# New slot tables for the state-space layer of a two-layer network on one Trainium2 core: 32 half slots, other row pairs on GpSimd, its row copies at other places

## What is computed

```python
def _ssm_forward(x, in_proj_w, conv_w, conv_b, x_proj_w, dt_proj_w, dt_proj_b, A_log, D_param, out_proj_w):
    ...
    h = _silu(h.transpose(0, 2, 1))            # after a causal convolution of 4 taps
    x_dbl = h @ x_proj_w
    dlt, Bm, Cm = (x_dbl[..., :dt_rank], x_dbl[..., dt_rank:dt_rank + n], x_dbl[..., dt_rank + n:])
    delta = jax.nn.softplus(dlt @ dt_proj_w + dt_proj_b)
    deltaA = jnp.exp(jnp.einsum('bld,dn->bldn', delta, A))
    deltaB_u = (delta * h)[..., None] * Bm[:, :, None, :]
    def step(state, t):
        dA_t, dBu_t, c_t = t
        state = dA_t * state + dBu_t
        y_t = jnp.einsum('bdn,bn->bd', state, c_t)
        return (state, y_t)
    ...
    y = ys.transpose(1, 0, 2) + h * D_param
    y = y * _silu(res)
    return y @ out_proj_w
```

## Time and profile before

| | |
|---|---|
| time, median of 3 runs | 4811.3 us (4810.6 to 4814.64) |
| profiled execution, its own time | 4813.99 us |
| span of the profile (first to last instruction) | 4812.0 us |
| the third phase, first to last slot table | about 4087 to 4812 us |
| one step of the loop | 41.0 us |
| in such a step: VectorE, TensorE, ScalarE, GpSimd busy | 36.2, 35.9, 30.1, 19.7 us |

### The profile page before, as it was taken

How to read it: one execution, slowest core, us unless ns; L and a number is a source line. 1 busy time by engine, 2 the same in 40 slices (tenths; PEclk the granted TensorE clock), 3 DMA queues, 4 the chain that set the end, 5 groups by cost and what they waited for, 6 DMA issues and landing times. The chain is left out here.

```text
span 4812.0 us, 130689 instructions
## 1 busy us (share of the span) xinstructions
PE 4274.3 (89%) x45166; PEld 3170.2 (66%) x45166; DVE 3900.2 (81%) x6890; ACT 3764.5 (78%) x11543; POOL 3537.5 (74%) x2504
## 2 busy tenths in 40 slices
PE   6988699998999899998999989999899997688887
PEld 3555477776777777776777767777677776355553
DVE  4776788888888888888888888888888885588887
ACT  2555588888888888888888888888888886677774
POOL 0100799988899888998989988899899995344444
PEclk9999799999999999999999999999999998788888
DMA  1000111111111111111111111111121111000000
GB/s 26 6 5 2 50 48 44 44 38 53 52 44 38 50 45 53 38 44 44 51 47 44 44 44 46 52 43 39 44 53 44 38 44 28 2 4 3 3 3 5
DMA packets 118630, 169.29 MB, mean 35 GB/s; under 512 B 26563, under 2 KB 44422, under 8 KB 118022
## 3 DMA queue, kind: packets, MB, share of 16 engines
q1 hardware_dynamic: 109246, 160.92, 12.6%
q10 hardware_dynamic: 8776, 0.45, 0.1%
HBM read 20.79 MB, written 2.10 MB: 5 GB/s over the span
## 5 line engine op out<-in xcount | busy, mean ns | idle before, releaser
L1375 POOL TENSOR_TENSOR b_w<-b_w,b_vt 128x512 f32<-128x512 f32 x768 | 1158.3, 1519 | 317.4 <-DVE b_vt L1289 191.6
L1379 POOL TENSOR_TENSOR b_rn<-b_ssm,all_neg_half 128x16 f32<-128x16 f32 x384 | 1261.4, 3285 | 32.0
L1174 ACT ACTIVATE b_Pr<-ps,b_nm 128x96 f32<-128x96 f32 x3072 | 1002.6, 353 | 0.6
L1174 ACT ACTIVATION_READ_ACCUMULATOR b_Pr<-ps,b_nm 128x1 f32 x3072 | 677.2, 220 | 0.0
L1216 ACT ACTIVATE b_PT<-ps 96x512 f32<-96x512 f32 x768 | 457.9, 596 | 259.8 <-PE ps L1026 244.1
L1060 PE MATMUL ps<-b_Whi,b_xlo 128*128 128x512 f32 x1152 | 581.2, 505 | 47.9 <-DVE b_Wlo L1306 24.9
L989 PE MATMUL ps<-all_ident,b_w 128*128 128x128 f32 x3072 | 464.2, 282 | 134.8 <-ACT b_qkT L1144 65.9
L1287 DVE TENSOR_TENSOR b_w<-ps,until_b_rotab 128x512 f32<-128x512 f32 x768 | 525.0, 684 | 60.9 <-ACT b_sq L1193 57.2
L1026 PE MATMUL ps<-all_ident,b_Pr 128*96 128x128 f32 x3072 | 488.5, 283 | 82.3 <-ACT b_PT L1216 44.2
L1193 ACT ACTIVATE b_sq<-ps 128x512 f32<-128x512 f32 x768 | 476.3, 620 | 59.7 <-PE ps L1062 49.1
L1289 DVE TENSOR_TENSOR b_vt<-ps,until_b_rotab 128x512 f32<-128x512 f32 x768 | 523.0, 681 | 0.0
(11 more groups left out here) (259 smaller groups left out, 9403.8 us busy)
## 6 DMA issues: line engine op xcount, KB each, us to landing
b_V<-b_Vraw SPq DMA_DIRECT2D x384, 192.0 KB, 2.6
b_V<-b_Vraw SPq DMA_DIRECT2D x384, 128.0 KB, 2.3
b_V<-b_Vraw SPq DMA_DIRECT2D x192, 64.0 KB, 2.2
b_Wraw<-in_L_ffn_Wqkv SPq DMA_DIRECT2D x36, 256.0 KB, 3.4
b_Wo<-in_L_ffn_Wo SPq DMA_DIRECT2D x6, 512.0 KB, 4.1
a_xtok<-in_L_attn_hidden_states SPq DMA_DIRECT2D x16, 128.0 KB, 2.1
out<-c_xout SPq DMA_DIRECT2D x16, 128.0 KB, 1.8
b_W<-in_L_ffn_W SPq DMA_DIRECT2D x6, 341.0 KB, 3.3
```

Source lines behind the costliest of these rows:

```text
L1174: last = nc.scalar.activation(s.Pr[:, r % 2, j, i], ps[:, S_BANK[j], i * KEYS:(i + 1) * KEYS], ACT.Exp, bias=s.nm[:, r, j, i:i + 1], accum ...
L1375: nc.gpsimd.tensor_tensor(rows, rows, s.vt[:, i % 4], ALU.add).then_inc(s.pool_add, 1)
L1379: nc.gpsimd.tensor_tensor(s.rn[:, j], s.ssm[:, j], g.neg_half[:, 0:HB], ALU.pow).then_inc(s.pool_r, 1)
```

## The change

All engines now run over 32 slots (`C_SLOTS`), and every table is new. GpSimd takes the pairs B0, B2, B4, C2, C3, C4 instead of B0, B3, B4, C1, C3, C4; six products as before. TensorE's waits ahead of B0, B1, C0 and C1 are new: they wait for the product of pair 6 or 7 of the item before. No operation is added or dropped, so what changes is the order on each engine. By the tables and the order of the `if` statements the new orders of a whole step are:

- VectorE: x3, B1, xbc, B3, scan 0, delta/du, moments 1, y, C0, x4, B5, C1, B6, B7, moments 2, scan 1, C5, C6, C7, x5. Before: B1, x3, xbc, B2, scan 0, delta/du, y, moments 1, C0, x4, B5, moments 2, B6, B7, C2, scan 1, C5, C6, x5, C7.
- GpSimd: B0, B2, statistics 1, copy of x3, B4, C2, statistics 2, C3, C4. Before: B0, B3, statistics 1, B4, C1, copy of x3, statistics 2, C3, C4.
- ScalarE: rows B0, dlt, rows B2, z, softplus, out, x3, rows B4, 4 exponentials, apply 1, rows C2, hT, 6 exponentials, x4, 10 exponentials, apply 2, xp, 8 exponentials, rows C3, hT2, rows C4, 4 exponentials, silu, lin. Before, apply 2 stood behind 20 exponentials as well, with xp, hT2 and rows C3 right behind it, and then 7 exponentials, lin, rows C4.
- TensorE: B0, B1, B2, xd, B3, sum 4', B4, sum 5', dl, sum 6', sum 7', B5, out, C0, x3, B6, C1, op, C2, h, x4, B7, in, sum 0, sum 1, C3, C4, h2, conv, sum 2, C5, C6, lin, sum 3, C7 (sums with a prime are those of the item before). Before: B0, B1, xd, B2, B3, sum 4', sum 5', sum 6', B4, dl, C0, out, x3, B5, sum 7', B6, op, C1, C2, x4, h, B7, sum 0, sum 1, in, C3, h2, lin, C4, C5, conv, sum 2, C6, C7, sum 3.

```diff
 PAIRS = NS // 2
-POOL_B, POOL_C = (0, 3, 4), (1, 3, 4)
+C_SLOTS = 32
+POOL_B, POOL_C = (0, 2, 4), (2, 3, 4)
...
-PE_B = {0: (0, 1), 1: (2, 3), 3: (4,), 8: (5,), 9: (6,), 10: (7,)}
-PE_C = {6: (0,), 9: (1, 2), 11: (3,), 12: (4, 5), 13: (6, 7)}
-PE_SUM = {10: (0,), 11: (1,), 13: (2,), 14: (3,), 17: (4, 5), 18: (6,), 24: (7,)}
-PE_OUT, PE_XD, PE_X3, PE_DL, PE_OP, PE_X4, PE_H, PE_IN, PE_H2, PE_CONV, PE_LIN = 7, 0, 7, 3, 9, 9, 10, 11, 11, 12, 12
-DVE_B_AT = {0: (1,), 3: (2,), 7: (5,), 8: (6, 7)}
-DVE_C_AT = {6: (0,), 11: (2,), 13: (5, 6), 15: (7,)}
-DVE_SCAN = {4: 0, 12: 1}
-DVE_X3, DVE_XD, DVE_Y, DVE_STATS1, DVE_X4, DVE_DELTA, DVE_STATS2, DVE_X5 = 3, 3, 5, 6, 7, 5, 8, 13
-ACT_ROWS = {0: (0,), 1: (1,), 3: (2,), 9: (3,), 12: (4,), 15: (5,)}
-ACT_OUT, ACT_X3, ACT_Z, ACT_SOFTPLUS, ACT_X4, ACT_APPLY1, ACT_HT, ACT_XP, ACT_APPLY2, ACT_HT2, ACT_SILU, ACT_DLT, ACT_LIN = 2, 2, 1, 2, 10, 6, 11, 11, 11, 11, 15, 0, 15
-FACTOR_SLOT = {4: (0, 2), 10: (2, 8), 11: (8, 20), 12: (20, 27), 15: (27, 32)}
-POOL_AT = {1: (0, 1), 5: (2,), 9: (3,), 13: (4,), 14: (5,)}
-POOL_X3, POOL_STATS1, POOL_STATS2 = 12, 1, 12
+PE_B = {1: (0, 1, 2), 2: (3,), 3: (4,), 10: (5,), 17: (6,), 20: (7,)}
+PE_C = {11: (0,), 17: (1,), 18: (2,), 22: (3, 4), 23: (5,), 25: (6,), 31: (7,)}
+PE_SUM = {21: (0,), 22: (1,), 23: (2,), 30: (3,), 34: (4,), 37: (5,), 40: (6,), 41: (7,)}
+PE_OUT, PE_XD, PE_X3, PE_DL, PE_OP, PE_X4, PE_H, PE_IN, PE_H2, PE_CONV, PE_LIN = 11, 1, 16, 7, 18, 19, 19, 20, 22, 22, 28
+DVE_B_AT = {8: (1,), 10: (3,), 19: (5,), 22: (6,), 23: (7,)}
+DVE_C_AT = {14: (0,), 20: (1,), 28: (5, 6), 29: (7,)}
+DVE_SCAN = {11: 0, 27: 1}
+DVE_X3, DVE_XD, DVE_Y, DVE_STATS1, DVE_X4, DVE_DELTA, DVE_STATS2, DVE_X5 = 4, 10, 13, 13, 16, 12, 26, 29
+ACT_ROWS = {0: (0,), 2: (1,), 6: (2,), 15: (3,), 28: (4,), 30: (5,)}
+ACT_OUT, ACT_X3, ACT_Z, ACT_SOFTPLUS, ACT_X4, ACT_APPLY1, ACT_HT, ACT_XP, ACT_APPLY2, ACT_HT2, ACT_SILU, ACT_DLT, ACT_LIN = 5, 5, 2, 5, 20, 14, 15, 22, 22, 28, 30, 1, 31
+FACTOR_SLOT = {7: (0, 2), 12: (2, 4), 19: (4, 10), 21: (10, 20), 23: (20, 26), 27: (26, 28), 30: (28, 32)}
+POOL_AT = {0: (0,), 1: (1,), 21: (2,), 27: (3,), 29: (4,), 31: (5,)}
+POOL_X3, POOL_STATS1, POOL_STATS2 = 12, 5, 28
...
                     for i in PE_B.get(slot, ()) if step.states else ():
                         if i == 0:
                             pe.wait_ge(s.xd_ready, 2 * n + 2)
-                        if i >= 2 and i - 2 in POOL_B:
-                            pe.wait_ge(s.rows_ready, N_POOL * n + POOL_B.index(i - 2) + 1)
-                        elif i >= 2:
-                            pe.wait_ge(s.bu_dve, len(DVE_B) * n + DVE_B.index(i - 2) + 1)
+                        before, of = (i - 2, n) if i >= 2 else (PAIRS + i - 2, n - 1)
+                        if before in POOL_B:
+                            wait(pe, s.rows_ready, N_POOL * of + POOL_B.index(before) + 1)
+                        else:
+                            wait(pe, s.bu_dve, len(DVE_B) * of + DVE_B.index(before) + 1)
...
```

More of the change, by code:

```diff
@@ L1516, in body @@
                     copy_mod(s.md_tail, 1, known(t), 2, 6).then_inc(s.md_tail_ready, 1)
-                for slot in range(SLOTS):
+                for slot in range(C_SLOTS):
                     if step.inner and slot == DVE_STATS1:
@@ L1738, in body @@
                         last.then_inc(s.op_full, 1)
-                    for at, item, there in ((slot, n, step.states), (slot + SLOTS, t, step.tail)):
+                    for at, item, there in ((slot, n, step.states), (slot + C_SLOTS, t, step.tail)):
                         for i in PE_SUM.get(at, ()) if there else ():
@@ L1747, in body @@
                                 for c in range(CC):
-                                    nc.tensor.matmul(ps[:, Y_BANK, c * NT:(c + 1) * NT], s.D_diag[:, c], s.h[:, own if at < SLOTS else other, c], start=False, stop=False, skip_group_check=True)
+                                    nc.tensor.matmul(ps[:, Y_BANK, c * NT:(c + 1) * NT], s.D_diag[:, c], s.h[:, own if at < C_SLOTS else other, c], start=False, stop=False, skip_group_check=True)
                             if i == PAIRS - 1:
@@ L1768, in body @@
                     for i in PE_C.get(slot, ()) if step.states else ():
[L1769 to L1772, removed]
+                        before, of = (i - 2, n) if i >= 2 else (PAIRS + i - 2, n - 1)
+                        if before in POOL_C:
+                            wait(pe, s.rows_ready, N_POOL * of + len(POOL_B) + POOL_C.index(before) + 1)
+                        else:
+                            wait(pe, s.yc_dve, len(DVE_C) * of + DVE_C.index(before) + 1)
                         spread(C_BANK[i % 2], 1, i).then_inc(s.c_full, 1)
```

## The result

The changed kernel takes 4971.5 us (median of 4 runs, 4968.14 to 4977.95) against 4811.95 us before (4 runs): a ratio of 1.0325, 95% interval 1.0313 to 1.0338. It is 160 us slower. The forecast was 4923 us, 111 more than before, with a range up to 4965. The sign came as forecast, and so did the lock that the forecast named as the cause; the size was 48 us short. The profiled execution took 4977.95 us, with a span of 4976.0, which is 6.5 above the median.

The account below looks back on a forecast made before the run. No engine was full: a 41.0 us step was taken as a ring of waits. Steps of 9.8 + 0.1 + 20.6 + 18.4 = 48.9 us added 112 with the end steps, giving 4923 us, range 4870 to 4965.

Parts of the forecast that it names:

- the lock: Scan 1 holds SBUF against GpSimd's second norm, ready 9.8 us after scan 1 starts; with its stall 85%.
- end of scan 0 to scan 1: VectorE from delta to scan 1: 9.8 us of unchanged work plus 0.1 idle.
- scan 1 to C5: VectorE's C5 begins 20.6 us after scan 1; 17.4 with full clock throughout, 21.6 with a late clock.
- C5 to scan 0: VectorE does C5 (1.2 us), then 8.07 of work as before; C7 waits 0.45 for TensorE.
- Rival 1: GpSimd's four norm instructions all get through between scan 1's two instructions: step 42.5 us, time 4833; chance 6%.
- rival 2: Faster, as scan 1 begins late enough to miss the norm: step 39.0 to 40.1 us, time about 4790; chance 5%.
- Who waits: ScalarE's apply 2 waits 7.5 us for the norm, TensorE stands at h2, and the convolution takes 7 at half clock.
- the upper bound: Half clock at the out projection, late clock behind sum 2 and the second path: 10.3 us a step, time 4958.
- The second path: TensorE's B3 spread waits for the B1 product, with softplus behind it: costs 0 to 0.3 us a step.
- x4: VectorE idle ahead of x4, as y begins later and only C0 fills the time: 0.1 to 1.2 us, 0.1 taken.
- The sum: A step grows 7.8 us to 48.9; 13 steps give 101, step 14 about 8, the last about 3: together 112.

Follow-up runs that it names:

- one entry: The kernel before with only VectorE's second moments moved directly ahead of scan 1 (slot 12 for 8): 4934.6 us.
- The fills: The changed kernel with unread matrix products in TensorE's gaps, 8 ahead of B3, 3 ahead of B6, 11 ahead of h2: 4911.95 us.
- the fills and the moments together: The changed kernel with moments 2 ahead of B6 and unread matrix products ahead of B3 (8) and B6 (3), none ahead of h2: 4868.1 us.
- the three moves: The changed kernel with moments 2 ahead of B6, B1 ahead of x3 and x5 ahead of C7: 4845.6 us, ratio 1.0069.

## Why the forecast was right in sign and short in size

| stretch, us | forecast | after, two steps in turn |
|---|---|---|
| end of scan 0 to scan 1 | 9.9 | 13.46, 14.81 |
| scan 1 to C5 | 20.6 | 18.25, 18.53 |
| C5 to scan 0 | 9.7 | 11.44, 11.45 |
| scan 0 | 8.7 | 8.74, 8.74 |
| step | 48.9 | 51.9, 53.5 |

The last row adds up the column; from scan 1 to scan 1, which takes the first stretch of the next step, the trace has 53.2 and 52.4.

**The lock: right, with other instructions held.** The forecast had L332 and L333 held. In the rows L332 always passed, and L333 with L335, or L335 with L337, were held, as the scan began 0.20 or 0.33 us late. The time came out nearly the same: the norm was to be ready 9.8 us after the scan's start, or 9.0 if the scan was late by 0.2 to 0.4; it was ready at 9.5 and 8.7. Rival 1 (all four between the two scan instructions) and rival 2 (the lock misses the norm) did not happen, except that one step of ten came near to rival 2. The runs show it both ways: one entry costs the kernel before 120 us, and moments 2 moved back by four slots take 86 from the changed one.

**Who waits: right, and somewhat too long.** Apply 2 waited 7.2 (7.5 forecast), C5 9.50 (9 to 13 forecast). The convolution was taken at half clock throughout, 7 us; it took 5.04 and 6.10, since the clock came back in the middle of it. This and the norm make the way from scan 1 to C5 (c in the forecast) 18.4 instead of 20.6: the forecast charged 2.2 us a step too many here. Its own terms also add up otherwise than it wrote: 11.4 + 7 + 1.9 + 0.6 is 20.9, and with sum 2 at half clock too (3.8) it is 22.8, where the upper bound took 21.6. So redone, the upper bound lies some 16 us higher, near 4974, above the measured time; but it would have got there by a stretch that in fact came out shorter.

**The second path: the step that failed.** The forecast named it, B3's spread waiting for the B1 product with sum 4', dl, z and softplus behind, and gave it "0 to 0.3". It had added up these instructions at the durations of before, at full clock. But TensorE stands idle 3.91 us ahead of that spread, and what follows it first runs at half clock: from B3's spread (4340.53) to z (4348.22) passed 7.7 us where 5.2 were taken, and in the step after (4392.42 to 4401.35), where the clock came back later, 8.9. With 5.4 for z to softplus, the 10.6 became 13.1 and 14.3, and delta waited 2.2 and 3.5. The fills confirm it: with the clock at 1.00 this wait is 0.46. The forecast asked of the long stall whether the clock would fall, and not of this second wait that the change adds on the same engine.

**x4: mis-sized by choice.** The bounds were 0.1 to 1.2 us and 0.1 was taken. It was 1.16: the out projection ran at half clock (2.04 us, as in the earlier trace rows). Together with the second path and the scan's own start this stretch came 3.6 and 4.9 us longer than forecast.

**C5 to scan 0: a term left out.** "What lay between C6 and scan 0 before, 8.07" took over x5 at 0.48 and md_tail at its short duration. GpSimd's B0 product now runs beside both, and they take 1.19 and 1.00 (VectorE's rows of after stand above): the stretch is 1.7 us longer than forecast. The two as they were before, then GpSimd beside them after:

```profile
4301.17 0.48 DVE L1554 SCALAR_TENSOR_TENSOR c_x5T<-c_tmp,c_md_tail,c_x4T 128x256 f32<-128x256 f32 x1
4302.76 0.17 DVE L1509 TENSOR_SCALAR c_md_tail<-all_mod 128x4 f32 x1
...
4386.98 5.32 POOL L1600 TENSOR_TENSOR c_bu<-c_du,c_rows 128x512 f32<-128x512 f32 x4 [2.49 <-ACT c_rows L1633]
```

The earlier trace rows had shown that the lock works in this direction; the forecast used it for the norm alone. Putting x5 one place earlier gave back 22 us, part of it by C7's wait; md_tail stayed held.

**The sum.** From the 12 loop steps and the one behind them, 13 in all, the trace has 678.2 us where before has 534.5: 144 more, and 101 were forecast (11.1 a step against 7.8). The last step of scans gave 7.9 against 8, and what stands behind the last scan 1 gave 2.7 against 3. The first step gave 3.1, where nothing was forecast. The remaining 6.5 us between the two profiled executions lie ahead of the first scan 1: the third phase began 6.3 us later (4093.8, before 4087.4), behind phases that the change doesn't touch, and the profiled execution of after is 6.5 above its median. The upper bound of 4958 held only 0.3 us at the second path and nothing for x5 and md_tail, which is why the range ended under the result.

**Not settled.** Why the fills and the moments together don't give the sum of the two is read from the rows of that run (C3's product under the scan, a gap and the clock behind it); it wasn't tried with that product moved out of the scan, or with that gap filled. The 34 us left behind the three moves were read off the rows and not taken apart by runs.

## What to carry to other kernels

A tiny GpSimd instruction that comes up together with a long VectorE instruction with two operands in SBUF can be held for the whole of the long one (here 0.2 us became 4.4). Leave the time that such a group needs (here 1.4 us) between the two, or let nothing urgent stand behind whoever waits for it. When a change adds a wait on TensorE, price the work behind that wait at half clock as well, for every gap and not for the longest alone; here the clock was at half behind gaps of 2.3, 2.4, 3.9 and 5.4 us. And when an order changes, list again which VectorE instructions run beside GpSimd products: a duration taken from before holds only with the same neighbour.

## What the runs showed of the hardware

- When both have work queued that wants SBUF, VectorE and GpSimd alternate instruction by instruction. Between the two instructions of a scan GpSimd got exactly one in, so a chain of four small ones (1.39 us) took 9.5 us; which of the four are held hangs on 0.1 to 0.4 us of the scan's start (0.20 late: L333 and L335; 0.33: L335 and L337; 0.56: L337 alone, and the step is 7 us shorter).
- A VectorE instruction with one tensor operand took longer too: md_tail, a TENSOR_SCALAR of 128x4 from SBUF to SBUF, took 1.00 us beside a GpSimd product and 0.17 with none beside it. The Trainium skill (SBUF — State Buffer, "Who interferes with whom") says that VectorE in a two-port mode contends with GpSimd, and that TENSOR_SCALAR can enter such a mode; the row agrees with that, though no run shows which mode md_tail ran in. The forecast had told only of two operands.
- TensorE's clock fell in gaps as short as 2.3 us: it was at 1.00 up to a gap of 2.40 us (with B1 ahead of x3) and up to one of 2.31 (moments and fills), and at 0.50 and 0.53 in the 2 us behind them.
- Useless work can pay: 22 short products a step on an idle TensorE made the changed kernel 60 us faster than it was without them, though it stayed 2% behind the kernel before.
